# Reciprocal root of the edge finish moved from GpSimd to ScalarE and VectorE, with four result buffers

## The reference

```python
x = _layernorm(x + _L0_gnn_ref(...), axis=-1)
x = _layernorm(x + _L1_gnn_ref(...), axis=-1)
x = _layernorm(x + _L2_gnn_ref(...), axis=-1)
x = _layernorm(x + _L3_gnn_ref(x, edge_index, ...), axis=-1)

def _layernorm(x, axis=-1, eps=1e-05):
    m = jnp.mean(x, axis=axis, keepdims=True)
    v = jnp.var(x, axis=axis, keepdims=True)
    return (x - m) / jnp.sqrt(v + eps)
```

## Time and profile before

| | us |
|---|---|
| median of 3 runs (4628.96 to 4634.05) | 4633.51 |
| the profiled execution, its own time | 4636.57 |
| its span | 4634.4 |
| first load of `finish_edges` issued at | 4450.38 |
| last scatter issued, ends at | 4624.60 |

### The profile page before, as it was taken

The page is one execution under the profiler, slowest core; times in us unless marked ns, Lnnn a source line. Parts: engine busy times, 40 slices in busy tenths (PEclk is TensorE's granted clock), DMA queues, the critical chain, the costliest instruction groups (busy, mean ns, idle before and its releaser), DMA issues. The chain is left out here.

```text
span 4634.4 us, 61427 instructions
## 1 busy us (share of the span) xinstructions
PE 3559.5 (77%) x14977; PEld 2219.4 (48%) x14977; DVE 3407.8 (74%) x10458; ACT 2211.6 (48%) x4450; POOL 3222.0 (70%) x2802
## 2 busy tenths in 40 slices
PE   5677777747777566489979999998688758687975
PEld 3465555534444466444435555554343357564321
DVE  7777877755666688755546888888766669797964
ACT  1366666632333477623327777777122313123742
POOL 1377878757777588677747888888588766462557
PEclk9888989879999787799989999999899979898988
DMA  3344444432333467534433333333333258695863
GB/s 92 95 126 117 123 116 128 121 99 80 96 96 91 130 205 208 170 114 140 135 112 107 125 125 125 125 125 117 102 109 107 86 178 254 160 193 144 279 197 111
DMA packets 463592, 621.19 MB, mean 134 GB/s; under 512 B 71541, under 2 KB 220204, under 8 KB 463308
## 3 DMA queue, kind: packets, MB, share of 16 engines
q1 hardware_dynamic: 402700, 534.09, 37.1%
q0 software_dynamic: 54912, 83.37, 8.3%
q10 hardware_dynamic: 5696, 0.55, 0.1%
HBM read 402.95 MB, written 218.46 MB: 134 GB/s over the span
## 5 line engine op out<-in xcount | busy, mean ns | idle before, releaser
L1180 PE MATMUL ps<-big,Whh 128*128 128x512 f32 x1176 | 540.1, 595 | 33.5 <-DVE big L1198 30.9
L697 PE MATMUL ps<-W2b,hid 128*128 128x128 f32 x1568 | 249.3, 326 | 197.6 <-DVE rN L882 197.6
L1605 PE MATMUL ps<-big,We 128*128 128x512 f32 x800 | 356.2, 599 | 5.0 <-DVE big L1755 3.8
L697 PEld LDWEIGHTS ps<-W2b,hid 128*128 128x128 f32 x1568 | 236.4, 236 | 234.9 <-issue 233.1
L1180 PEld LDWEIGHTS ps<-big,Whh 128*128 128x128 f32 x1176 | 212.2, 190 | 254.3 <-issue 251.4
L1213 POOL TENSOR_TENSOR big<-big 128x512 f32<-128x512 f32 x196 | 251.6, 1303 | 73.0 <-ACT big L1207 73.0
L712 ACT ACTIVATE hid<-ps,b 128x512 f32<-128x512 f32 x196 | 134.0, 686 | 300.0 <-PE ps L690 290.0
L594 POOL DMA_INDIRECT me<-node_tab,ix x208 | 217.4, 1045 | 72.7 <-issue 52.8
L1755 DVE SCALAR_TENSOR_TENSOR big<-r2N,zN 128x512 f32<-128x512 f32 x400 | 252.7, 685 | 16.2 <-DMA r2N<-type_row 6.4
L601 POOL DMA_INDIRECT meta<-me,rank_ix x208 | 214.1, 1030 | 63.1 <-issue 60.6
L1605 PEld LDWEIGHTS ps<-big,We 128*128 128x128 f32 x800 | 151.5, 192 | 188.3 <-issue 182.5
(11 more groups left out here) (403 smaller groups left out, 10744.3 us busy)
## 6 DMA issues: line engine op xcount, KB each, us to landing
xN<-x_tab SPq DMA_DIRECT2D x196, 256.0 KB, 3.0
h_tab<-yN SPq DMA_DIRECT2D x124, 256.0 KB, 2.3
krow<-key_row SPq DMA_DIRECT2D x100, 256.5 KB, 4.3
agg<-in_xt SPq DMA_DIRECT2D x98, 256.0 KB, 3.2
big<-x_tab SPq DMA_DIRECT2D x98, 256.0 KB, 3.1
x_tab<-hid SPq DMA_DIRECT2D x98, 256.0 KB, 3.5
agg<-x_tab SPq DMA_DIRECT2D x98, 256.0 KB, 2.8
x_tab<-zN SPq DMA_DIRECT2D x98, 256.0 KB, 2.0
```

Of the source, the lines that this page charges most:

```text
L697: last = nc.tensor.matmul(OUT0[:, spans[j]], hid1[g % 2][:, c, spans[j]], W2b[:, c, :], start=(c == 0), stop=(c == 1))
L1180: last = nc.tensor.matmul(bank[:, :], Whh[:, l, c * D:(c + 1) * D], h, start=True, stop=not both)
L1605: last = nc.tensor.matmul(MS[:, :], We[:, l * NTYPE + t, :], masked[g % 2][:, t, :], start=(t == 0), stop=(t == NTYPE - 1))
```

## The change

GpSimd no longer computes the reciprocal root. ScalarE takes the square root of the variance plus epsilon, and VectorE its reciprocal, followed by one Newton step (three more operations on a tile of 128x4), which leaves rstd. GpSimd keeps the scatters alone. The result has four buffers in place of two (zN and rN), with four semaphores. On ScalarE the list of one round k is now the root of group k and then the normalising of group k-1. On VectorE the four new operations of group k-1 stand between scale of k and shift of k-1. The small tiles `root`, `guess` and `error` live in the buffers veq, rsq and shq, which are free in this stage.

```diff
@@ -3092,15 +3092,16 @@
         def finish_edges():
 
             ph = Phase()
-            scaled_x, scaled_1, scaled_2, sum_d, st_d, mv_d, eps_d, rstd_d, shift_d, out_d = ph.sems(10)
+            scaled_x, scaled_1, scaled_2, sum_d, st_d, mv_d, eps_d, root_d, guess_d, square_d, error_d, rstd_d, shift_d, out_d = ph.sems(14)
             x_in, one_in, two_in = (ph.sems(2) for _ in range(3))
-            stored = sca_a
+            stored = [*sca_a, *sca_b]
             per = 16 * J
             xe, d1, d2 = x2N[0], x2N[1], [big[:, 4 + u, :].rearrange("p (j d) -> p j d", j=J) for u in range(2)]
             px, p1, p2 = xb, yN, r2N
-            result = zN
+            result = [*zN, *rN]
             SUM = PS[0:2]
             st, mv, ve, rs, sh = norm_bufs[0]
+            root, guess, error = (t.rearrange("p (k j) -> p k j", k=2) for t in (veq[0][:, :], rsq[0][:, :], shq[0][:, :]))
             spans = [slice(j * P, (j + 1) * P) for j in range(J)]
             with nc.Block() as block:
 
@@ -3118,21 +3119,13 @@
 
                 @block.gpsimd
                 def _(pool):
-                    def power(g):
-                        after(pool, eps_d, g)
-                        nc.gpsimd.tensor_tensor(rs[g % 2][:, :, 0], ve[g % 2][:, :, 0], mhalf[:, 0:J], ALU.pow).then_inc(rstd_d, 1)
-
-                    def scatter(g):
+                    for g in range(EGR):
                         after(pool, out_d, g)
                         for j in range(J):
-                            nc.gpsimd.indirect_dma_start(out, at_index(IX_DSTW, g + EDGE0, j), result[g % 2][:, j, :], None,
-                                                         bounds_check=N - 1, oob_is_err=False).then_inc(stored[g % 2].sem, 16)
-
-                    for k in range(EGR + 1):
-                        staged(k, EGR, power)
-                        staged(k - 1, EGR, scatter)
-                    for u in range(2):
-                        landed(pool, stored[u], per * ((EGR + 1 - u) // 2))
+                            nc.gpsimd.indirect_dma_start(out, at_index(IX_DSTW, g + EDGE0, j), result[g % 4][:, j, :], None,
+                                                         bounds_check=N - 1, oob_is_err=False).then_inc(stored[g % 4].sem, 16)
+                    for u in range(4):
+                        landed(pool, stored[u], per * ((EGR + 3 - u) // 4))
 
                 @block.tensor
                 def _(pe):
@@ -3150,16 +3143,39 @@
 
                 @block.scalar
                 def _(act):
-                    for g in range(EGR):
+                    def square_root(g):
+                        after(act, eps_d, g)
+                        after(act, guess_d, g - 2)
+                        nc.scalar.activation(root[:, g % 2, :], ve[g % 2][:, :, 0], ACT.Sqrt).then_inc(root_d, 1)
+
+                    def normalise(g):
                         u = g % 2
                         after(act, shift_d, g)
-                        after2(act, stored, g - 2, per)
-                        for j in range(J):
-                            last = nc.scalar.activation(result[u][:, j, :], SUM[u][:, spans[j]], ACT.Identity, scale=rs[u][:, j, :], bias=sh[u][:, j, :])
+                        if g >= 4:
+                            landed(act, stored[g % 4], per * (g // 4))
+                        for j in range(J):
+                            last = nc.scalar.activation(result[g % 4][:, j, :], SUM[u][:, spans[j]], ACT.Identity, scale=rs[u][:, j, :], bias=sh[u][:, j, :])
                         last.then_inc(out_d, 1)
+
+                    for k in range(EGR + 1):
+                        staged(k, EGR, square_root)
+                        staged(k - 1, EGR, normalise)
 
                 @block.vector
                 def _(dve):
+                    def inverse(g):
+                        u = g % 2
+                        y, t, v = guess[:, u, :], error[:, u, :], ve[u][:, :, 0]
+                        after(dve, root_d, g)
+                        nc.vector.reciprocal(y, root[:, u, :]).then_inc(guess_d, 1)
+                        after(dve, guess_d, g)
+                        nc.vector.tensor_tensor(t, y, y, MUL).then_inc(square_d, 1)
+                        after(dve, square_d, g)
+                        nc.vector.scalar_tensor_tensor(t, t, -0.5, v, MUL, MUL).then_inc(error_d, 1)
+                        after(dve, error_d, g)
+                        after(dve, out_d, g - 2)
+                        nc.vector.scalar_tensor_tensor(rs[u][:, :, 0], t, 1.5, y, ADD, MUL).then_inc(rstd_d, 1)
+
                     def scale(g):
                         u = g % 2
                         after(dve, sum_d, g - 2)
@@ -3200,10 +3216,11 @@
                         staged(k - 1, EGR, moments)
                         staged(k - 1, EGR, eps)
                         staged(k, EGR, scale)
+                        staged(k - 1, EGR, inverse)
                         staged(k - 1, EGR, shift)
 
-            for u in range(2):
-                stored[u].end(per * ((EGR + 1 - u) // 2))
+            for u in range(4):
+                stored[u].end(per * ((EGR + 3 - u) // 4))
 
         sorted_pool(0)
         coefficients(0)
```

## The result

The change made the kernel slower: a median of 4679.2 us (4 runs, 4674.93 to 4682.57) against 4631.55 (4 runs, 4628.96 to 4634.05). The ratio is 1.0103, with a 95% interval of 1.0091 to 1.0115: 47.6 us more, where 56 were forecast. The profiled execution took 4679.02 us, at the median; that of the kernel before took 4636.57, 5.0 us above its median, so the two profiles differ by less than the medians.

The account below looks back on a forecast made before the run. The prediction took GpSimd, 6.28 us a group, as the bound. The loop's 17.4 us less 2.4 at the end, plus 41 for the clock, gave 56 us more: 4689.5 us, whole range 4646 to 4712.

Parts of the forecast that it names:

- The moved instruction decides the sign: On ScalarE, root(g+1) ahead of normalise(g) makes each eps wait for the one before through TensorE's group: slower, 0.92.
- The loop of 7.03 us: Eps, root, four activations, TensorE's sums, statistics, next eps: 7.03 us a group against 6.28, last eps 17.4 us later.
- The clock, 41 us: TensorE's granted clock falls after its pause in each group: 1.8 us for each of 23 groups, 41 us.
- The end, 2.4 us back: From last eps to last scatter: 12.3 us in place of 14.5, giving back 2.2 to 2.5, taken as 2.4.
- VectorE's additions and the four buffers cost nothing: VectorE's 0.8 to 1.55 us a group hidden under TensorE's sums; four buffers remove ScalarE's wait for landings, at no cost.
- The table load costs nothing: On ScalarE before root 0: one load of 1.28 us, root ready at 1.7 us after eps, wanted at 1.9.
- the 4540.97 group: A group of the kernel before on TensorE, 4540.97 to 4546.41: 5.44 us with a lower clock, 1.67 more than 3.77.
- the dearer price: A group of the kernel before on TensorE, 4573.51 to 4579.85: 6.34 us, 2.57 more, after the 3.99 us wait.
- a clock that holds: Rival, chance 0.12: TensorE's clock stays up despite the pauses and only the loop is paid, +15 us, 4648.5.
- The open loop: Rival, chance 0.06: normalise(g) still runs under the sums of g+1, GpSimd's 5.2 us sets the pace, -29 us, 4604.
- A clock that is low almost always: Rival, chance 0.10: TensorE's pauses leave no time to recover, 78 us more than the loop, +93 us, 4727.
- a table load with each switch: Rival, chance 0.02: ScalarE loads tables twice a group between root and normalising, at least +59 us over the loop's 15.

Follow-up runs that it names:

- e1_order: The changed kernel with ScalarE normalising group k-1 before it takes the root of group k: 4600.98 us, ratio 0.9940 to the kernel before.
- e2_sums: The changed kernel with four PSUM tiles for the sum in place of two, ScalarE's order as in the change: 4601.49 us, ratio 0.9936.
- e3_wait: The kernel before with one more wait, ScalarE normalising group g only when eps of g+1 is there: 4665.39 us, ratio 1.0080.
- e4_busy: The changed kernel with two idle matmuls ahead of TensorE's wait in each group from the third on: 4654.04 us, ratio 1.0042.
- e9_busy_eps: The changed kernel with two idle matmuls a group from the third on, and eps as a scalar_tensor_tensor: 4705.49 against 4695.32 us, ratio 1.0023.
- e8_no_newton: The changed kernel without the Newton step, the reciprocal of the root being rstd itself: 4754.3 us against 4703.99 for the kernel before, ratio 1.0100.
- e6_buffers: The kernel before with four result buffers and nothing else changed: 4702.26 against 4703.99 us, ratio 0.9994.
- e5_busy_before: The kernel before with two idle matmuls ahead of TensorE's wait in each group from the third on: 4702.03 against 4703.99 us, ratio 0.9994.

## Why the prediction was right

The sign, the cause and its place were as forecast: 4679.2 us within 4646 to 4712 and within the forecast's own range of 4668 to 4711. Step by step:

- *The moved instruction decides the sign.* Shown from three sides: the order alone undone (e1_order), the other link of the loop cut (e2_sums), and the loop put into the kernel before without anything else (e3_wait).
- *The loop of 7.03 us.* Measured 6.93. The root pushes the activations back by 0.12, not 0.15, and from the first matmul to the statistics it is 3.73, not 3.77. This gave 15.1 us in place of 17.4.
- *The clock, 41 us.* The mis-sized term: it measured 31.5. The count was nearly right (19 of 23 groups, where five of seven to all were allowed for), but a slowed group cost 31.5 / 19 = 1.66 us on average, the price of the 4540.97 group (1.67), which makes 1.37 for each of the 23 where the forecast took 1.8. TensorE's waits were 3.23 to 3.52, and no wait of 3.99 came. But the length of the wait does not give the price: 18 of the 19 slowed groups cost 1.4 to 1.7, after waits of 3.23 to 3.52, and one, from the eps at 4602.48 to that at 4612.41, cost 3.0 after a wait of 3.23, more than the dearer price of 2.57. e4_busy and e9_busy_eps show that the lower clock is what this term pays for.
- *The end, 2.4 us back.* Measured 2.0. The last eps came at 4654.90, not near 4668: 2.7 us are the earlier start, and the rest is the two terms above.
- *VectorE's additions and the four buffers cost nothing.* Nothing is seen of either in e8_no_newton and e6_buffers, within the 8 us that their intervals leave. The reciprocal of four columns takes 170 ns, near the lower bound.
- *The table load costs nothing.* It ran at 4443.81, 14 us before the first root: it does not wait for eps, so neither the row's 1.28 us nor the 2.66 us of the Trainium skill (ScalarE: Activation LUTs, "What ACT_TABLE_LOAD costs") could matter. Whether a drain follows a load can't be told from this, since ScalarE had nothing to do.
- *Not foreseen:* eps held up by a scatter, 0.29 us in three groups here (0.9 us), in nearly all of e4_busy. The kernel before has it too, where GpSimd sets the pace: seven of its eps take 0.22 to 0.43 us.

Of the rivals, a clock that holds is what e9_busy_eps shows by force (1.0023, 11 us over the kernel before, where 15 were worked out; its idle matmuls are not in the changed kernel). The open loop is what e1_order shows: 4601 us, where 4604 were given as the faster side. So these two prices were right within 4 us on these chips; on the third chip the open loop brought 11 us, not 29. A clock that is low almost always (93 us) did not come: 19 of 23 groups were slowed, each for a part of its sums. Nor did a table load with each switch: there was one load in all. The prices of these two were not tested.

## What to carry to other kernels

When an operation moves to another engine, write down what now stands ahead of what in that engine's list, and follow each wait once round: a step of group g+1 put ahead of the last step of group g turns a pipeline into a loop if any buffer of group g is wanted back for g+2. Either the order or one more pair of buffers mends it; here each took 78 us off. And the lower clock that followed TensorE's pauses cost nothing that could be told while GpSimd set the pace (e5_busy_before), and some 31 of the 48 us once TensorE was in the loop.

## What the hardware showed unexpectedly

- A tensor_scalar of 128x4 from SBUF to SBUF on VectorE took 0.45 us in place of 0.17 when it started about 0.5 us into a scatter of GpSimd, and ended with it. In the kernel before it took 0.43, 0.34 and 0.22 when it started 0.54, 0.62 and 0.75 us into a scatter of 0.97, so it ended with the scatter there too. The same value by a scalar_tensor_tensor took 0.16 at the same place. The Trainium skill (SBUF — State Buffer, "SBUF: two separate sides") says that VectorE and GpSimd share a pair of ports, locked for a whole instruction, and that a VectorE operation in a two-port mode wants it. The slow form fits that if it runs in such a mode, which no trace here shows. The same sentence counts an operation with two SBUF inputs as well, but only against a GpSimd instruction that reads SBUF; the scalar_tensor_tensor has two (the variance twice) and was not held up. A tensor_scalar that started 0.3 us into a scatter (4470.01, scatter from 4469.72) was not held up, nor was one that started 0.49 us into it in the kernel before (4470.79, scatter from 4470.30), which the sentence alone does not explain. Nor is this the only such moment: in e1_order eps took 0.23 to 0.24 us where it started 0.03 to 0.04 us ahead of a scatter.
- The same kernel before took 4632.6, 4704.0 and 4695.3 us on three chips, and on the third the kernel with the order mended had delays of VectorE in nine groups that it did not have on the first. The gain of that version is 32 us on one chip and 11 on another.
